# In 3 of 24 steps of a scan unit, VectorE scans into PSUM and multiplies the states with C itself; GpSimd did it in all 24, and the places of the work beside the scan move

## The reference, cut to what matters

```python
Bproj = x @ W_B + b_B;  Cproj = x @ W_C + b_C
delta = softplus(x @ W_D + b_D + p_Delta)
dA = delta[..., None] * A
A_bar = exp(dA)
B_bar = (A_bar - A) / dA * delta[..., None] * Bproj[:, :, None, :]
def step(h, inp):                       # over the tokens
    a, b, c, xl = inp
    h = a * h + b * xl[..., None]
    y = einsum('bn,bdn->bd', c, h)      # 16 states n of each of 768 channels d
    return (h, y)
h = h + ssm(layernorm(h));  h = h + experts(layernorm(h))
```

## Time and profile before

| | before |
|---|---|
| median of 3 runs | 11202.05 us |
| profiled execution, its time and its span | 11207.42 us, 11205.8 us |
| PE / DVE / ACT / POOL busy in the span | 9064.0 / 6392.5 / 4405.5 / 6423.6 us |
| mean granted TensorE clock | 0.879 |
| `tail`'s steps on GpSimd | from 5410 us to about 11100 us |
| POOL `weigh_in` and `weigh_out` | 672 each, 4000 and 4005 ns |
| DVE `weigh` and `scan` with a kept state | 2688 and 2304, 666 and 1143 ns |

### The profile page before, as it was taken

The page is one execution under the profiler, slowest core; times in us unless marked ns, Lnnn a source line. Parts: engine busy times, 40 slices in busy tenths (PEclk is TensorE's granted clock), DMA queues, the critical chain, the costliest instruction groups (busy, mean ns, idle before and its releaser), DMA issues.

```text
span 11205.8 us, 91659 instructions
## 1 busy us (share of the span) xinstructions
PE 9064.0 (81%) x31004; PEld 4193.3 (37%) x31004; DVE 6392.5 (57%) x8141; ACT 4405.5 (39%) x7002; POOL 6423.6 (57%) x2484
## 2 busy tenths in 40 slices
PE   7888888888879999995577787787777877877876
PEld 5446446446434444441133332332333333323332
DVE  1331331331332222222688888888888888888885
ACT  3334334333323333331344444444444444444443
POOL 0000010010116544440699999999999999999986
PEclk9999999999989999995788888888888888888888
DMA  1111111111114333321222323333223233232231
GB/s 50 30 32 49 29 39 43 29 45 37 39 43 94 83 82 81 81 64 31 93 89 100 113 86 109 105 103 103 97 100 109 87 104 111 94 112 97 100 104 57
DMA packets 404136, 856.33 MB, mean 76 GB/s; under 512 B 78131, under 2 KB 330308, under 8 KB 396310
## 3 DMA queue, kind: packets, MB, share of 16 engines
q1 hardware_dynamic: 367750, 761.86, 22.5%
q0 software_dynamic: 21712, 51.75, 2.1%
q10 hardware_dynamic: 14336, 38.54, 1.0%
HBM read 623.41 MB, written 209.04 MB: 74 GB/s over the span
## 4 chain that ended last, share of the span: by engine, by line
DVE 14%; POOL 14%; PE 11%; issue 9%; ACT 3%; DMA 0%; SPq 0%; DVEq 0%; POOLq 0%
POOL v L1362 9%; DVE v L1703 6%; DVE v L1694 6%; POOL v L1352 5%; PE ps L1497 5%; PE ps L1394 1%; PE ps L1498 1%; PE ps L1500 1%; DVE dl L1685 1%; PE ps L1399 1%; PE ps L1401 1%; PE ps L1437 1%; ACT ps L1593 1%; DVE gm L1771 0%; ACT gm L1618 0%
## 5 line engine op out<-in xcount | busy, mean ns | idle before, releaser
L1352 POOL TENSOR_TENSOR v<-xr,bt 128x1792 f32<-128x1792 f32 x672 | 2687.9, 4000 | 342.6 <-PE ps L1437 246.1
L1593 ACT ACTIVATE ps<-dr,aa 128x448 f32<-128x448 f32 x2688 | 1698.7, 636 | 2830.3 <-DVE v L1703 2781.3
L1362 POOL TENSOR_TENSOR v<-v,ct 128x1792 f32<-128x1792 f32 x672 | 2691.6, 4005 | 128.7 <-ACT st L1583 128.7
L1703 DVE TENSOR_TENSOR_SCAN v<-ps,st,v 128x448 f32<-128x448 f32 x2304 | 2632.6, 1143 | 0.0
L1694 DVE SCALAR_TENSOR_TENSOR v<-ps,aa,v 128x448 f32<-128x448 f32 x2688 | 1791.3, 666 | 738.4 <-POOL v L1352 548.8
L242 POOL DMA_DIRECT2D tokens<-ob x448 | 239.3, 534 | 3070.4 <-DVE ob L469 3019.0
L1437 PE MATMUL ps<-v,dg 128*32 128x448 f32 x5376 | 718.0, 625 | 396.1 <-POOL v L1362 396.1
L1497 PE MATMUL ps<-w_or_w,gm 128*112 128x384 f32 x1792 | 755.8, 574 | 305.0 <-ACT ot L1627 200.0
L1497 PEld LDWEIGHTS ps<-w_or_w,gm 128*112 128x112 f32 x1792 | 352.8, 207 | 664.1 <-ACT ot L1627 261.2
L768 PE MATMUL ps<-xt,wa 128*128 128x448 f32 x1344 | 586.2, 570 | 0.0
L1484 PE MATMUL ps<-wpb 9*128 9x448 f32 x224 | 172.7, 893 | 485.8 <-DVE gm L1771 338.8
(11 more groups left out here) (324 smaller groups left out, 15240.0 us busy)
## 6 DMA issues: line engine op xcount, KB each, us to landing
xr<-h_by_channel SPq DMA_DIRECT2D x168, 896.0 KB, 4.8
dr<-delta_by_channel SPq DMA_DIRECT2D x168, 896.0 KB, 5.3
x<-tokens SPq DMA_DIRECT2D x252, 224.0 KB, 4.8
tokens<-ob POOLq DMA_DIRECT2D x448, 112.0 KB, 2.3
w_or_w<-in_w SPq DMA_DIRECT2D x29, 1536.0 KB, 6.6
w_or_w<-centred_w SPq DMA_DIRECT2D x27, 1536.0 KB, 7.0
h_by_channel<-h SPq DMA_DIRECT2D x112, 336.0 KB, 10.8
delta_by_channel<-dl SPq DMA_DIRECT2D x112, 336.0 KB, 4.9
```

What stands on the lines that cost most here:

```text
L1352: tt(v[:, n % RING], xr[:, dc % 2], bt[:, q:q + 1, :].to_broadcast([128, 4, T]), ALU.mult).then_inc(s_v, 1)
L1362: tt(v[:, n % RING], v[:, n % RING], ct[:, q:q + 1, :].to_broadcast([128, 4, T]), ALU.mult).then_inc(s_cm, 1)
L1593: fn(bank((4 * n + g) % 3), dr[:, dc % 2, g, :], ACT.Exp, scale=aa[:, 4 * k + g:4 * k + g + 1]).then_inc(s_a, 1)
L1703: nc.vector.tensor_tensor_scan(v[:, n % RING, g, :], bank((4 * n + g) % 3), v[:, n % RING, g, :], 0.0 if first else st[:, 4 * k + g:4 * k ...
```

## The change

1. Steps 5, 13 and 21 of a unit (`OWN`) are done another way. VectorE's scan writes into the PSUM bank that held the exponentials, not into v. VectorE then copies the last column to the kept states (128x1), and multiplies the bank by C into v (128x448). It waits for its own scan ahead of the copy, and for the copy and the product ahead of raising `s_sc`. GpSimd's `weigh_out` and ScalarE's `keep_states` are left out in these steps.
2. The semaphores count only what still passes (`others`), with three new ones for the own steps (`s_sp`, `s_cv`, `s_sv`); TensorE and the DMA that reloads C wait for the one or the other.
3. Numbers of the table move: the expert work comes one or two steps earlier (P_IN 6 to 5, V_IN 10 to 9, A_GL 15 to 14), B and C too (P_BC 12 to 9, V_BC 16 to 14); the masks and the eight outputs are spread over more steps, and A_OUT ends at 27, not 25. A_HW, P_PJ, A_RS, P_SQ, V_DL and A_MX stay.

```diff
+OWN = (5, 13, 21)
+def others(n):
+    i, k = divmod(n, STEPS)
+    return i * (STEPS - len(OWN)) + sum(j not in OWN for j in range(k + 1))
+def owned(n):
+    return n + 1 - others(n)
...
-        P_PJ, P_MU, P_VAR, P_Z, P_BC = 1, 7, (8, 10), 11, 12
+        P_PJ, P_MU, P_VAR, P_Z, P_BC = 1, 7, (8, 10), 11, 9
...
-        A_OUT = (22, 22, 23, 23, 24, 24, 25, 25)
+        A_OUT = (21, 22, 23, 23, 24, 25, 26, 27)
...
             def weigh_out(i, k):
                 dc, q = divmod(k, Q)
+                if k in OWN:
+                    return
...
-                pool.wait_ge(s_st, n + 1)
+                pool.wait_ge(s_st, others(n))
...
-                pe.wait_ge(s_cm, n + 1)
+                if k in OWN:
+                    pe.wait_ge(s_cv, 4 * owned(n))
+                else:
+                    pe.wait_ge(s_cm, others(n))
...
             def keep_states(i, k):
+                if k in OWN:
+                    return
...
                 if k == V_BC:
+                    dve.wait_ge(s_rs[0], i + 1)
...
+                if k not in OWN:
+                    nc.vector.tensor_tensor_scan(row, a, row, start, ALU.mult, ALU.add).then_inc(s_sc, 1)
+                    return
+                nc.vector.tensor_tensor_scan(a, a, row, start, ALU.mult, ALU.add).then_inc(s_sp, 1)
+                dve.wait_ge(s_sp, 4 * owned(n) + g - 3)
+                cp(st[:, 4 * k + g:4 * k + g + 1], a[:, T - 1:T]).then_inc(s_sv, 1)
+                tt(row, a, ct[:, k % Q, :], ALU.mult).then_inc(s_cv, 1)
+                dve.wait_ge(s_sv, 4 * owned(n) + g - 3)
+                dve.wait_ge(s_cv, 4 * owned(n) + g - 3)
+                dve.sem_inc(s_sc, 1)
```

More of the change, by code:

```diff
@@ L1189, in tail @@
         s_cm = sem("t_states_times_c")
+        s_sp = sem("t_own_states_scanned")
+        s_cv = sem("t_own_states_times_c")
+        s_sv = sem("t_own_last_states_kept")
         s_ns = sem("t_states_summed")
@@ L1206, in tail @@
         s_out = [sem("t_out_stored_even"), sem("t_out_stored_odd")]
-        P_PJ, P_MU, P_VAR, P_Z, P_BC = 1, 7, (8, 10), 11, 12
+        P_PJ, P_MU, P_VAR, P_Z, P_BC = 1, 7, (8, 10), 11, 9
         A_HW, A_MU, A_SQ, A_RS, A_MX, A_SP = 5, 11, (9, 13), 14, (16, 17), (17, 18)
[L1210 to L1213, removed]
-        A_OUT = (22, 22, 23, 23, 24, 24, 25, 25)
-        V_VAR, V_ENC, V_IN, V_LOG, V_EQ, V_OH, V_MASK = 7, 9, 10, 11, 13, 15, (18, 18, 19, 19)
-        ROUTE, TAIL = 9, 26
+        V_Z, V_BC, V_DL = 15, 14, (18, 19)
+        P_SQ, P_MEAN, P_ENC, P_IN, P_LOG, P_TURN = (0, 2), 1, 4, 5, 6, 10
+        P_MASK, P_OUT = (12, 13, 14, 15), (16, 17, 18, 18, 19, 20, 21, 22)
+        A_SQ2, A_MS, A_RS2, A_EX, A_GL = (2, 4), 5, 7, 11, 14
+        A_OUT = (21, 22, 23, 23, 24, 25, 26, 27)
+        V_VAR, V_ENC, V_IN, V_LOG, V_EQ, V_OH, V_MASK = 6, 8, 9, 10, 12, 14, (16, 17, 18, 19)
+        ROUTE, TAIL = 9, 28
         def pair_bank(o):
@@ L1286, in spread_c @@
                 if i < UNITS:
-                    after(sp, s_cm, STEPS * (i - 1) + STEPS - Q + q + 1)
+                    k = STEPS * (i - 1) + STEPS - Q + q
+                    if i >= 1 and k % STEPS in OWN:
+                        sp.wait_ge(s_cv, 4 * owned(k))
+                        sp.wait_ge(s_cm, others(k))
+                    elif i >= 1:
+                        sp.wait_ge(s_cm, others(k))
+                        sp.wait_ge(s_cv, 4 * owned(k))
                     spread_row(ct[:, q, :], i, 1, q).then_inc(s_lc[q], 16)
@@ L1700, in scan @@
                 if g == 0 and not first:
-                    dve.wait_ge(s_st, n + 1 - STEPS)
+                    if k in OWN:
+                        dve.wait_ge(s_sv, 4 * owned(n - STEPS))
+                    else:
+                        dve.wait_ge(s_st, others(n - STEPS))
                 dve.wait_ge(s_wt, 4 * n + g + 1)
-                nc.vector.tensor_tensor_scan(v[:, n % RING, g, :], bank((4 * n + g) % 3), v[:, n % RING, g, :],
-                                             0.0 if first else st[:, 4 * k + g:4 * k + g + 1], ALU.mult,
-                                             ALU.add).then_inc(s_sc, 1)
+                a = bank((4 * n + g) % 3)
+                start = 0.0 if first else st[:, 4 * k + g:4 * k + g + 1]
+                row = v[:, n % RING, g, :]
+                if k not in OWN:
[8 more added lines that the diff above has]
+                dve.sem_inc(s_sc, 1)
             def step(i, k):
```

## The result

| | before | after |
|---|---|---|
| median (range, runs) | 11203.12 us (11201.44 to 11207.72, 6) | 11379.1 us (11376.26 to 11387.23, 6) |
| span of the profiled execution | 11205.8 us | 11377.1 us |
| mean granted TensorE clock | 0.879 | 0.877 |
| a full unit, typical (mean of 25) | 204.8 (204.30) us | 211.6 (211.14) us |

The changed kernel takes 1.0157 times as long [1.0144, 1.017]. The forecast was 11374 with a range of 11180 to 11480. Times are in us throughout, and a number in square brackets behind an instruction is the time that its engine stood idle before it.

The account below looks back on a forecast made before the run. GpSimd was taken as fullest, the binding engine changing by stretch: output products then GpSimd, GpSimd then TensorE, VectorE. -7.5 + 7.2 + 6.9 = +6.6 us a unit, +172 over 26 periods, gave 11374 us, range 11180 to 11480.

Parts of the forecast that it names:

- A: Stretch V22 to V28, 6 steps, 56.2 us before, bound by output products and copies, then GpSimd: 7.5 us gained.
- B: Stretch V28 to V13, 9 steps, 74.2 us before; TensorE would be late to the token means: 7.2 us lost.
- C: Stretch V13 to the next V22, 9 steps, 74.4 us before, bound by VectorE: 6.9 us lost.
- V22: Start of VectorE's step 22; other Vk likewise, V28 being step 4 of the next unit.
- a mean product that starts later: Start of B: TensorE's mean product at V28 + 0.9, before at V28 - 0.7; 1.6 us lost.
- the third expert product: In B: P_IN's new place puts a third expert product ahead of the token means on TensorE, 4.8 us more.
- the copy and router that moved into step 12: End of B: fourth copy and router's second half move into step 12, V12 to V13 takes 8.0; 0.9 us more.
- Rival 1: TensorE does not hold B, VectorE alone sets it: B gains 5.8, unit 6.4 us shorter, 11036 us; chance 0.15.
- The wait for the inverse deviation: In C, step 14: VectorE's B and C work waits 3.0 us behind the gelu, which cost 1.42 before; 1.6 more.
- 2 (no change): Full clock for product 3, own steps at lower bound, mean product starting as before: +0.1 a unit, 11205 us; chance 0.07.
- 3 (1.3 a group): Slower still: own-step groups at 1.3 us, 3.6 more in C, 10.2 a unit, 11467 us; chance 0.10.
- 4 (GpSimd keeps the pace): VectorE has cover everywhere, so GpSimd's relief counts fully: 12 us a unit gained, 10890 us; chance 0.02.

Follow-up runs that it names:

- e2: Kernel before with all new places of the changed table, the wait ahead of B and C work included, but no own steps: 11115.89 us, ratio 0.9921.
- e3: Kernel before with only the output products and their copies at the new places, no own steps, experts and router as before: 10969.76 us, ratio 0.979.
- e4: Changed kernel with own steps and new output places, but expert work, router and B and C work at the old places: 11236.93 us, ratio 1.0031.
- e6: Changed kernel with ScalarE's output copies one place earlier where they can be (A_OUT 21, 21, 22, 22, 23, 24, 25, 26): 11241.24 us, ratio 1.0034.
- e1: Changed kernel with own steps 5, 13 and 21 but all numbers of the table as before: 11445.26 us, ratio 1.0218.
- e10: Kernel before with outputs at the new places, ScalarE's output copies earlier than in the change, and one own step, at 5: 11016.54 us, ratio 0.9832.
- e5: Changed kernel with the gelu and its table loads back at ScalarE's step 15 (A_GL 15 for 14): 11354.9 us, ratio 1.0135.
- e8: Kernel before with outputs at the new places, ScalarE's output copies earlier than in the change, and one own step, at 0: 10939.84 us, ratio 0.9764.

## Why the prediction was right

The time, the sign and all three parts came out (A -6.8, B +7.2, C +6.4 for -7.5, +7.2, +6.9), but inside B two terms were wrong and cancelled, which was luck.

**A, right in total.** Squares and product 3 wait for copies as said. Product 3 with what hangs on it took 8120.52 - 8113.30 = 7.2, the forecast's number. It started at V22 + 5.5, not 4.6, because the last group of step 21 lies behind V22; so V24 came at V22 + 17.9 for 17.0, and the four steps after it took 31.5 for 31.7. What the forecast did not say is where the 5.1 us of idling ahead of product 3 come from: from the own step at 21 and the late copy together. Without own steps (e2, e3) product 3 waits 2.0 at most and takes 2.83 or up to 4.5, with A at 46.4 or 47.4. With them (e4) it waits 5.1 and takes 4.2 to 5.5, with A at 48.0 to 49.6. With them and the early copies (e6) it doesn't wait, takes 2.74, and A is 43.4.

**B, right in total, wrong in two terms.** The forecast had 1.6 for a mean product that starts later, 4.8 for the third expert product, 0.9 for the copy and router that moved into step 12, and nothing for own step 5.
- The start: the squares began where they were put, at V28 - 3.25, but took 4.85, not 3.1, and the sum of states 1.5 behind them; the mean product came at V28 + 3.0. Yet e6 has no late squares, and its B is not shorter than after but equal or longer: this term is 0 in the changed kernel. The forecast took "Waits within I leave as they are" and 66.3 us as a fixed length. It isn't: what starts late runs at full clock (4.78 for 6.16), and the third projection waits for ScalarE's copy of h until V28 + 23.0, whatever TensorE did before.
- The earlier expert work: e2 against e3 gives 80.0 - 74.2 = 5.8, and 4.8 + 0.9 was said. V12 to V13 took 8.0 as forecast. No run takes the product apart from the other moves of its group, but the timelines do: from the start of the third projection to the end of the token means TensorE takes 48.9 in the changed kernel and in e2, and 44.4 in before, and the one thing more in it is an expert product, whose follower starts 4.6 behind it. In e2, where nothing is waited for in between, the start of the mean product does count: it lies at V28 + 2.4 to 2.8, and B is 79.7 to 80.1 with it.
- Own step 5: 1.5 (e1, e4, most units), 1.4 (after against e2) and 1.5 or 3.1 (e10) for 0. Of ScalarE's copies only that of the second projection makes TensorE wait, once in a unit. Where the wait is long, the low clock of the third projection adds another 1.6.

The end of the token means, 8226.57 + 2.57, is V28 + 71.9; the forecast had 72.0. Rival 1 (11036) needed it by V28 + 59.0 and falls.

**C, size of the own step.** The own step is 3.9, not 3.4. In the timeline of after, one group of step 21:

```profile
8099.94 0.66 DVE L1723 SCALAR_TENSOR_TENSOR v<-ps,aa,v 128x448 f32<-128x448 f32 x1
8100.52 1.15 DVE L1741 TENSOR_TENSOR_SCAN ps<-ps,st,v 128x448 f32<-128x448 f32 x1
8101.70 0.16 DVE L1743 COPY st<-ps 128x1 f32<-128x1 f32 x1
8101.77 0.62 DVE L1744 TENSOR_TENSOR v<-ps,ct 128x448 f32<-128x448 f32 x1
8102.52 0.68 DVE L1723 SCALAR_TENSOR_TENSOR v<-ps,aa,v 128x448 f32<-128x448 f32 x1
...
8110.42 0.69 DVE L1723 SCALAR_TENSOR_TENSOR v<-ps,aa,v 128x448 f32<-128x448 f32 x1
```

Four groups take 8110.42 - 8099.94 = 10.48 for 6.55, so 3.93 more, 0.98 a group for 0.85. Scan to copy (1.18) and copy to product (0.07) are near what was said; product to next weighing is 0.75 where 0.635 was, since the wait ahead of raising `s_sc` keeps these two apart. Two own steps less the group that ends behind V22 are 3.93 + 2.95 = 6.9, and what is left of C without them is 74.4 in e1 and e4, as before, and 73.9 in the changed kernel, as the 74.0 of e2. The wait for the inverse deviation was 3.00, as forecast. But e5 shows that its price over the gelu's old place is 0.7, not 1.6. This doesn't come of the own steps: e4 has them and the gelu at 15, and waits 1.42 as before. It comes of the router's last piece (V_OH), which moved from step 15 to 14. The gelu holds step 15 at 9.9 long in before, e4 and e5 alike, so VectorE waits by as much longer (2.19) as it has less to do there.

The masks were booked at nothing and gained 0.5. One of VectorE's four mask products now stands in step 17, and its 0.6 falls into the wait ahead of step 18 that was there anyway. First before, then after:

```profile
7992.83 0.68 DVE L1694 SCALAR_TENSOR_TENSOR v<-ps,aa,v 128x448 f32<-128x448 f32 x1 [2.39 <-ACT ps L1593]
```

```profile
8073.54 0.68 DVE L1723 SCALAR_TENSOR_TENSOR v<-ps,aa,v 128x448 f32<-128x448 f32 x1 [1.88 <-ACT ps L1621]
```

So C is 74.4 - 1.5 + 6.9 + 1.6 - 0.5 = 80.9, measured 80.8. Two own steps cost 1.1 more than said, but the last group of step 21 (1.0) lies behind V22 and so in A; what makes C 0.5 shorter than the forecast's 81.3 is the hidden mask product.

By the Trainium skill, VectorE: DVE Perf Modes, section on the DRAIN you can't avoid, a semaphore behind each of eight copies cost nothing extra. Carried over to the own step, that gave 2.8 in the prediction. The rows decide against carrying it over, with 3.9: in the own step each instruction waits for the one before it, and it loses the overlap with both neighbours.

**The ends.** 25 full units grew by 6.84 each, 171 us, which is the whole rise of the span. The 26th period, from the first unit to the second, grew by 11.2, where 8 gained at the start were to cancel 8 lost. The start (to V22 of the first unit) gained only 3.8, and 3.4 of that lie ahead of the first step, in the tokenizer, which the change doesn't touch and where the profiled runs differ by some 10 us (its end lies between 5404.9 and 5415.3). The last period gained 4.5 and what follows it 2.6. The forecast's 26 periods were right by luck at the ends.

**Rivals.** 2 (no change) needed own steps at the lower bound and the full clock for product 3, and neither came; its third condition, a late mean product that costs nothing, did hold. 3 (1.3 a group) falls by 0.98. 4 (GpSimd keeps the pace) falls by GpSimd's 33.2 us of idle time a unit. Of this last one e8 shows the true core: an own step is free where GpSimd is the one that everybody waits for, and 5, 13 and 21 are not such places.

Still open is why TensorE takes the low clock in some units and not in others after waits that hardly differ: product 3 in e2 is slow after 1.2, and in most units of e3 fast after 2.0.

## What to carry to other kernels

Taking work from the fullest engine pays only in the stretch in which that engine sets the pace: cut the period by what bounds it, and price the added work in each stretch by itself (here about 0, 1.5 to 3.1 and 3.9 us for the same step in three places). A stretch of an in-order engine that reads as full is no fixed length: a late start can be made up by a higher granted clock and shorter waits, and a delay of a neighbour's copy can stretch it. There can be a point in it that another engine fixes: what is gained or lost ahead of that point doesn't reach its end. A single unit can mislead: in e3, e6 and e10 one slow product or projection makes two kinds of unit, 1.0 to 1.6 us apart. Where one change holds two edits, time each alone: the gain of 231 us and the losses of some 250 and 145 stood in one diff.

## What the runs showed of the hardware

- A scan (128x448) that writes into PSUM took 1149 ns, one into SBUF 1140; a multiply of PSUM by SBUF 615, and a 128x1 copy out of PSUM 158. PSUM as a target costs 9 ns of 1149 here.
- A VectorE product and the next weighing, with a wait for the product between, start 0.75 apart at 0.62 long; independent neighbours overlap by 0.08 (8099.94 + 0.66 to 8100.52).
- Six passes of squares took 4.85 after 7.48 of idle, at a granted clock of 0.50 (the lower level, 1.2 GHz), and 2.52 in a busy stretch; the twelve passes behind the next 1.5 us took 4.78 at 1.00 (2.4 GHz).
- After shorter waits either level was seen: eight passes of an output product took 2.83 after 0.6 to 2.0 of idle in e3 and 4.53 after 1.2 to 2.0 in e2 (granted clock 1.00 and 0.62), and six passes of a projection 2.67 after 1.7 and 4.09 after 2.7 in e10 (1.00 and 0.61).
